# Flamingo block on one core: first keys ahead of the gate matmul, signed row ends in the table of maxima, dense matmuls behind the last projection

## The reference

```python
q = (x @ Wq); k = (context @ Wk); v = (context @ Wv)      # 16 heads of 32
attn = softmax(where(mask, q k^T * scale, max_neg)); xattn = (attn v) @ Wo
x = x + tanh(g_xattn[0]) * xattn(_layernorm(x), ctx, mask, ...)
# feed-forward:
scale = sigmoid(clip_x) * max(|layernorm(x)|) / 127       # one number for the whole tensor
xq = clip(round(y / scale), -128, 127) * scale
h = fake_quant(silu(xq @ gate^T) * (xq @ up^T))           # again one number for all of h
x = x + tanh(g_ffn[0]) * (h @ down^T)
```

## Time and profile before

| | |
|---|---|
| median of 3 runs | 616.19 us (615.35 to 618.91) |
| the profiled execution: time, span | 615.18 us, 613.4 us |
| TensorE busy | 599.6 us, 98% |
| VectorE busy | 518.3 us, 84% |
| ScalarE busy | 376.0 us, 61% |
| GpSimd busy | 234.9 us, 38% |
| attention, up, down begin | 0, about 370.0, about 530.3 us |

### The profile page before, as it was taken

The page is one execution under the profiler, slowest core; times in us unless marked ns, Lnnn a source line. Parts: engine busy times, 40 slices in busy tenths (PEclk is TensorE's granted clock), DMA queues, the critical chain, the costliest instruction groups (busy, mean ns, idle before and its releaser), DMA issues. The chain is left out here.

```text
span 613.4 us, 12115 instructions
## 1 busy us (share of the span) xinstructions
PE 599.6 (98%) x3727; PEld 446.5 (73%) x3727; DVE 518.3 (84%) x957; ACT 376.0 (61%) x484; POOL 234.9 (38%) x473
## 2 busy tenths in 40 slices
PE   8999999999999999999999997999999999899997
PEld 6799999999999999999999873444444444444544
DVE  6788899999999998999999877888888888856765
ACT  5554677777777777877775535555555554455653
POOL 6253454544544454544533112111011110067775
PEclk9999999999999999999999998999999999999999
DMA  8534785354434445534642000496642110199633
GB/s 318 172 117 119 197 193 115 84 106 89 89 89 95 95 84 109 113 70 112 139 92 61 27 1 10 114 229 219 210 173 67 35 34 1 45 368 399 251 120 120
DMA packets 118507, 77.89 MB, mean 127 GB/s; under 512 B 98211, under 2 KB 100669, under 8 KB 118461
## 3 DMA queue, kind: packets, MB, share of 16 engines
q1 hardware_dynamic: 113169, 60.51, 38.6%
q10 hardware_dynamic: 5292, 16.82, 7.4%
HBM read 32.48 MB, written 21.36 MB: 88 GB/s over the span
## 5 line engine op out<-in xcount | busy, mean ns | idle before, releaser
L1459 ACT ACTIVATE sb_silu<-ps_g,sb_sgu 128x512 f32<-128x512 f32 x88 | 60.5, 688 | 72.0 <-PE ps_g L1554 43.4
L1554 PE MATMUL ps_g<-sb_xqT,sb_wgu 128*128 128x512 bf16 x352 | 90.3, 379 | 0.6 <-DVE sb_xqT L1510 0.6
L1554 PE MATMUL ps_u<-sb_xqT,sb_wgu 128*128 128x512 bf16 x352 | 90.3, 379 | 0.0
L1525 DVE SCALAR_TENSOR_TENSOR sb_h<-ps_u,sb_sgu,sb_silu 128x512 f32<-128x512 f32 (+1 forms) x88 | 66.1, 751 | 19.8 <-PE ps_u L1554 19.3
L1074 PE MATMUL ps_q<-sb_xT_hi,sb_wq_hi 128*128 128x256 f32 x256 | 75.4, 294 | 0.7 <-DVE sb_xT_lo L764 0.6
L1635 POOL TENSOR_TENSOR sb_wgu<-sb_wgu,sb_x 128x512 f32<-128x512 f32 x31 | 53.6, 1730 | 52.6 <-DVE sb_wgu L1692 52.6
L632 ACT ACTIVATE sb_prob<-sb_prob 128x616 f32<-128x616 f32 x64 | 45.6, 713 | 44.3 <-DVE sb_prob L797 44.3
L1076 PE MATMUL ps_q<-sb_xT_hi,sb_wq_lo 128*128 128x256 f32 x256 | 72.4, 283 | 0.0
L1075 PE MATMUL ps_q<-sb_xT_lo,sb_wq_hi 128*128 128x256 f32 x256 | 72.3, 283 | 0.0
L1759 PE MATMUL ps_z<-sb_wdT,sb_hq 128*128 128x512 bf16 x330 | 71.9, 379 | 0.2
L1529 DVE TENSOR_REDUCE sb_hmax<-sb_h 128x1 f32<-128x512 f32 (+1 forms) x88 | 60.4, 686 | 7.6
(11 more groups left out here) (238 smaller groups left out, 1422.7 us busy)
## 6 DMA issues: line engine op xcount, KB each, us to landing
h_spill<-sb_h SPq DMA_DIRECT2D x4, 2816.0 KB, 9.5
sb_h<-h_spill ACTq DMA_DIRECT2D x16, 704.0 KB, 7.1
out_dram<-sb_wgu SPq DMA_DIRECT2D x31, 256.0 KB, 2.2
sb_x<-in_x_dram ACTq DMA_DIRECT2D x5, 1024.0 KB, 6.1
sb_w_in<-in_L_ffn_w_gate_dram SPq DMA_DIRECT2D x11, 256.0 KB, 2.8
sb_w_in<-in_L_ffn_w_up_dram SPq DMA_DIRECT2D x11, 256.0 KB, 2.6
sb_x<-in_x_dram SPq DMA_DIRECT2D x2, 1024.0 KB, 14.0
sb_x<-in_x_dram SPq DMA_DIRECT2D x2, 512.0 KB, 4.4
```

Of the source, the lines that this page charges most:

```text
L1459: act.activation(silu[(j * KI + i) % 2][:, :, :].rearrange("p t n -> p (t n)"), p_g[(j * KI + i) % 2][:, :], ACT.Silu, scale=sgu[:, i:i + ...
L1525: dve.scalar_tensor_tensor(steps_h, p_u[(j * KI + i) % 2][:, :, :], sgu[:, KI + i:KI + i + 1], silu[(j * KI + i) % 2][:, :, :], ALU.mult, ...
L1554: last = pe.matmul(banks[(j * KI + i) % 2][:, :], wgu[:, what, k, i * P:(i + 1) * P], xqT[j][:, k, :], start=(k == 0), stop=(k == KD - 1))
```

## The change

There are four edits. The matmul `p_gate` moves from ahead of the first keys to behind the last keys, and the two dense matmuls between it and the keys go away. `xmax` gets three more columns: the last row's four scaled, signed ends are written into columns 31 to 34, without the reduce that made one absolute value of them, and the reduce over the table in "up" takes absolute values. Twelve dense matmuls of 512 columns are added behind TensorE's last projection; they write `p_x`, which nobody reads by then. In "up" `keep_warm(2)` becomes `keep_warm(1)` and `keep_warm(6)` becomes `keep_warm(8)`.

```diff
-        xmax = sb("xmax", [P, NT])
+        xmax = sb("xmax", [P, NT + 3])
...
-                ends_n = sb("ends_n", [P, 2, 2])
...
                         dve.wait_ge(v_ends, 4)
                         dve.wait_ge(g_nb2, m + 1)
-                        dve.tensor_scalar(ends_n[:, :, :], ends[:, :, :], rs2[:, m:m + 1], nb2[:, m:m + 1],
-                                          ALU.mult, ALU.add).then_inc(v_ends, 1)
-                        dve.wait_ge(v_ends, 5)
-                        dve.tensor_reduce(xmax[:, m:m + 1], ends_n[:, :, :], mybir.AxisListType.XY, ALU.max,
-                                          apply_absolute_value=True).then_inc(v_xmax, 1)
+                        dve.tensor_scalar(xmax[:, m:m + 4], ends[:, :, :].rearrange("p a b -> p (a b)"),
+                                          rs2[:, m:m + 1], nb2[:, m:m + 1], ALU.mult, ALU.add).then_inc(v_xmax, 1)
...
-                    pe.wait_ge(l_small, 64)
-                    pe.wait_ge(v_mask, 3)
-                    pe.matmul(p_gate, ones_row, gate_row, start=True, stop=True).then_inc(t_gate, 1)
-                    warm_dense(2)
                     pe.wait_ge(v_ck, 1)
                     pe.wait_ge(l_wk, 16)
                     keys_part(0)
...
                     keys_part(3)
+                    pe.wait_ge(l_small, 64)
+                    pe.wait_ge(v_mask, 3)
+                    pe.matmul(p_gate, ones_row, gate_row, start=True, stop=True).then_inc(t_gate, 1)
...
                     tile_slots(pe, slot)
+                    for _ in range(12):
+                        last = pe.matmul(p_x[:, :, :].rearrange("p k n -> p (k n)"), identb[:, :],
+                                         identb[:, :].unsqueeze(1).broadcast_to([P, KD, P]), start=True, stop=True)
+                    last.then_inc(t_warm, 1)
...
-                    dve.tensor_reduce(am1[:, :], xmax[:, :], X, ALU.max).then_inc(v_am, 1)
+                    dve.tensor_reduce(am1[:, :], xmax[:, :], X, ALU.max, apply_absolute_value=True)\
+                       .then_inc(v_am, 1)
...
-                    keep_warm(2)
+                    keep_warm(1)
                     pe.wait_ge(g_one, 1)
                     pe.wait_ge(v_spread, 1)
                     pe.matmul(p_u[0][:, 0, :], ones[:, :], spread[:, :], start=True, stop=True).then_inc(t_am, 1)
-                    keep_warm(6)
+                    keep_warm(8)
```

## The result

| | before | changed |
|---|---|---|
| median of the runs | 615.64 us (5 runs, 615.35 to 618.91) | 619.25 us (5 runs, 618.16 to 619.76) |
| ratio, 95% interval | | 1.0046 [1.0023, 1.0068] |
| profiled execution: time, span | 615.18, 613.4 us | 619.37, 617.6 us |

Slower by 3.6 us in the median; the ratio, which goes by the means, says 2.8 us, 1.4 to 4.2 us by the interval. The forecast was 616.0 and a range up to 617.7.

The account below looks back on a forecast made before the run. The prediction took TensorE's gapless matmul queues to bound the kernel, with other engines setting the pace only in the opening and the seam. +0.10 - 0.20 - 0.13 = -0.23 us took the median from 616.19 to 616.0, range 614.5 to 617.7.

Parts of the forecast that it names:

- so the clock rose in between: Opening, TensorE: nine matmuls at 0.42 us each, the later pair at 0.22, read as the clock having risen between them.
- the clock falls in the opening: Rival: without the pair, TensorE's clock falls in the opening; about +1.2 us there, 617.1 in all; 6 in 100.
- the transposes of tile 2 would not move: Opening: keys end 0.76 us earlier, but these transposes wait for VectorE's low part of tile 1, so gain nothing.
- The +0.10: Opening: the gate matmul ahead of the first queries costs 0.32 us less 0.22 slack; bounds 0 to 0.32.
- The slack: End of the opening: queries(1) could start at 20.77 but starts at 20.99, behind VectorE's q_lo, leaving 0.22 us.
- -0.20 for the way to `am1`: End of attention's last row: without the reduce VectorE, last in the block, ends 0.20 us earlier; bounds 0 to 0.33.
- The clock at the seam: Between last projection and "up": the twelve matmuls keep TensorE at 2.4 GHz; gain 0.13 us, bounds 0 and 0.20.
- cost nothing at the barrier: Seam: the twelve matmuls take 2.64 us, over by about 369.2, hidden behind VectorE's end at 369.47.
- Forecast at 1.00 from 366 to 377: Sign expected in the profile after: granted clock of 1.00 through the seam.
- -0.13: Seam: the f32 matmul ahead of `amax` at full clock, 0.10 us, plus an earlier start, 0.03 us.
- keep_warm(8) "hidden": Seam, in "up": the eight take 1.76 us and end near 372.6, earlier than the six did, costing nothing.

Follow-up runs that it names:

- no_pair: The kernel before without the opening's two dense matmuls, the gate matmul staying ahead of the keys; median 615.91 us, ratio 1.0001 to before.
- best: The changed kernel with before's opening, GpSimd's `first_n[2]` waiting for VectorE's `spread`, and dense matmuls filling TensorE's holes in "up"; median 616.01 us, ratio 0.9999 to before.
- the later 24: Two further groups of twelve executions of the changed kernel, unchanged, after its first five; mean 616.86 us, medians 617.27 and 616.09 us.
- open_only: The kernel before with the opening edit alone: gate matmul behind the last keys, two dense matmuls gone; median 615.75 us, ratio 0.9989 to before.
- gate_late: The kernel before with the gate matmul moved behind the last keys and the two dense matmuls kept; median 615.48 us, ratio 0.9996 to before.
- after_order: The changed kernel with one more wait: GpSimd makes `first_n[2]` only when VectorE's `spread` is there; median 615.37 us.
- dense_only: The kernel before with only the twelve dense matmuls behind the last projection and keep_warm(1) and (8); median 616.10 us.
- open_17: The kernel before with seventeen dense matmuls at the start instead of nine; median 618.02 us, ratio 1.0020 to before.
- after_again: The changed kernel once more, unchanged, for twelve executions; median 617.27 us, ratio 1.0017 to before.

## Why the prediction was wrong

**The opening: the step that failed.** The prediction took the clock of the opening as a given of the kernel and put it into the sum at nothing. It compared the nine matmuls at 0.42 us with the pair at 0.22 and wrote "so the clock rose in between". That was one execution. Of the 15 profiled executions with nine dense matmuls, 12 had the clock up by about 9 us and three not before about 15 to 16 (the changed kernel, `no_pair`, `best`); those three have the twelve pick records in 2.56 us. So the executions part ahead of the first instruction that the change moves. The prediction had this as the rival "the clock falls in the opening", at 6 in 100 and +1.2 us; in truth it does not fall but fails to rise, at +3.4 us, and that before the first instruction that the change touches. `no_pair` and `best` have before's instructions on TensorE up to that point; before itself was not profiled with a late opening, but 24 of its 146 executions lie in the upper heaps. The span of its three runs, 615.35 to 618.91, stood in the prediction as noise around one value; most likely it was two kinds of opening.

**The falls at the first group and at down: the second step.** The prediction let both stages begin as before; the clock behind 377 has no term in it. In the 29 executions of the changed kernel a second stretch at half clock is there in ten, three of them among the first five, and costs 2.8 us against none by the later 24. So the first median of 619.25 was bad luck in two places, a draw with at least one late opening (the profiled one) and three double falls out of five.

**The rest of the opening.** That the transposes of tile 2 would not move held wherever the clock was up: from the transposes of tile 0 to those of tile 2 it took 3.48 us in before and 3.48 to 3.49 with gate or pair gone. The +0.10 was sized a little too small, its mechanism was right. With the gate between keys and queries it takes 5.42 us from those transposes to values_part(0), before 4.91: the gate costs 0.5 us there and not 0.32, since the queries start 1.98 us behind the last keys against 1.47. VectorE's q_lo ends 8.03 us after those transposes start, with the gate moved or not (8.02 in `open_only`, 8.03 in `gate_late`), so it does not stand behind TensorE, as the prediction said. The slack is 0.33 us and not 0.22, and queries(1) starts 8.35 us after them against 8.18: +0.18 us. In five other executions, two with the gate in its old place, q_lo itself ended 0.1 to 0.8 us later, and queries(1) with it. With the clock down, the keys are on the path and the edit gains: 4.79 us between the two transposes against 5.44 in `no_pair` and 5.95 in `best`.

**The removed reduce.** -0.20 for the way to `am1` was right (0.19). What came next was missed: `spread` meets GpSimd, which costs 0.60 us at full clock (a seam of 10.07 against 9.47 in `after_order`). The net is a loss of 0.40 (10.07 against 9.67 in `dense_only`).

**The clock at the seam.** Forecast at 1.00 from 366 to 377: so it was in the profile after. Worth -0.43 and not -0.13: 0.28 us come before `amax`, VectorE's whole wait of 0.20 and 0.07 because `amax` now begins that much ahead of the end of the row of `first_n[1]`; and 0.16 us come behind it (4.70 us to the first group against 4.86), where the prediction had nothing. Which step gives these 0.16 was not worked out, and the changed kernel takes 4.86 us there though its clock was up. Together with the 0.40 of the reduce, the clock's 0.43 makes the seam what it was. The twelve matmuls ended 0.4 us before VectorE and cost nothing at the barrier, as forecast.

**keep_warm(8) "hidden".** It was, but at full clock the last of the eight ends 3.2 us ahead of the first group (374.63 + 1.89 to 379.69), and with a part of the six at half clock it ended 2.7 us ahead. Behind it TensorE has only transposes and holes up to the first group, and there the clock fell in two profiled executions of kernels with keep_warm(8). That this is why they fell is argued; what is shown is that dense matmuls in these holes end it.

**Down.** 3.23 or about 4.57 us for the same code. It occurred in kernels with and without the change (`no_pair`, `open_17`), so the profile after charges it to the change wrongly. 71 of 146 executions of before have a second stretch at half clock.

**What stays open.** What decides in an execution whether the clock rises at 9 or at 16 us was not found; neither was whether the changed kernel's chance of the late opening differs from before's. How many of the first five had it is open too: two of them, the profiled one among them, have a single stretch at half clock and lie at 619.25 and 619.37, where the later ones with a single stretch reach 617.26, so they look like late openings; the three with two stretches do not tell, since `after_again` took 618.67 with an early opening and two stretches. That the mean is higher by 0.5 to 0.9 us agrees with two stretches in seven of the later 24. After_order kept the hole, had two stretches in one of twelve, and came out at 615.68 in the mean.

## What to carry to other kernels

Before pricing a change at a place where a clock or a lock is decided, look at how the executions of the unchanged kernel scatter: three runs 3.6 us apart on a 0.3 us effect say that a profile shows one of several courses. Split the executions by their mean granted clock, and the courses come apart. Read TensorE's clock from the pace of equal matmuls, twelve records in 1.34 or 2.56 us, and not only from the granted column. Keep-warm matmuls have to reach up to the work that they protect (here 36 of 36 executions kept the clock once they did), and a step that an engine saves may only bring it into another engine's lock: look at who runs at the new moment.

## What the hardware showed that was not expected

- The granted clock column gives 1.00 at the start of the program while 512 columns take 0.42 us each; in three profiles it does so up to about 16 us, at half the pace. Behind its first change (at 369 us in before) it agrees with the pace.
- Behind the same instructions the clock rose by about 9 us in 12 of 15 profiled executions and at about 16 us in three; some 3.4 us of 616 depend on it.
- VectorE's `spread`, 128 x 128 f32, takes 0.28 or 0.76 us beside the same instruction of GpSimd, and 0.29 us when that is held back. In both cases GpSimd's row starts 0.13 or 0.14 us after `am1`, so the starts do not show which of the two waits, only the durations do.
- A fall at a seam cost 0.43 us (idle engine waiting on others), at the first group 1.65 us and at the start of down 1.35 us, of which 0.5 us come back: the price is what stands in TensorE's queue at that time.
